# Graph network kernel: the first adjacency matrix built slab by slab beside its first product, the second one made by turning tiles on TensorE

## What is computed

```python
edge_index = jnp.stack([src, dst])
x = _layernorm(x + _L0_gnn_ref(...))   # 3 times: m = h @ weight[i]; agg = segment_sum(m[src], dst); h = gru_cell(agg, h)
x = _layernorm(x + _L1_gnn_ref(...))   # hypergraph: sums of h[src] at dst, then of those at src, batch norm
x = _layernorm(x + _L2_gnn_ref(...))   # attention: softmax over the edges of a src, sum of attn * mapped[dst] at src
x = _layernorm(x + _L3_gnn_ref(...))   # an MLP on each edge, segment sum at dst, an MLP on each node
```

## Time and profile before

| | |
|---|---|
| median of three executions | 5898.96 us (5894.77 to 5907.12) |
| profiled execution | 5895.11 us, of which the span from first to last instruction is 5893.0 us |
| busy: TensorE, GpSimd, VectorE, ACT | 69 %, 44 %, 38 %, 29 % of the span |
| mean granted TensorE clock | 0.864 of full speed |
| moved by DMA | 786.87 MB |

### The profile page before, as it was taken

The page is one execution under the profiler, slowest core; times in us unless marked ns, Lnnn a source line. Parts: engine busy times, 40 slices in busy tenths (PEclk is TensorE's granted clock), DMA queues, the critical chain, the costliest instruction groups (busy, mean ns, idle before and its releaser), DMA issues. The chain is left out here.

```text
span 5893.0 us, 80722 instructions
## 1 busy us (share of the span) xinstructions
PE 4074.7 (69%) x24696; PEld 3170.2 (54%) x24698; DVE 2255.1 (38%) x4547; ACT 1685.4 (29%) x2823; POOL 2578.0 (44%) x2583
## 2 busy tenths in 40 slices
PE   4960000000999998996999799679999577777777
PEld 2430000000787787874555455369999466666665
DVE  5993000000446446437000100547777633333333
ACT  0020000000555555543000100358877322222222
POOL 0037777777777777760000000000000377777772
PEclk9985555555999999998999899799999799999998
DMA  5929500000883883881666666114543111111111
GB/s 188 407 77 366 209 0 0 0 3 0 275 285 102 274 271 106 286 233 41 195 200 173 160 200 199 44 57 144 148 143 116 43 52 50 51 51 51 50 51 39
DMA packets 307968, 786.87 MB, mean 134 GB/s; under 512 B 100762, under 2 KB 116823, under 8 KB 307783
## 3 DMA queue, kind: packets, MB, share of 16 engines
q1 hardware_dynamic: 182152, 548.50, 30.2%
q10 hardware_dynamic: 43680, 177.21, 7.8%
q0 software_dynamic: 81952, 58.72, 4.5%
HBM read 599.36 MB, written 184.70 MB: 133 GB/s over the span
## 5 line engine op out<-in xcount | busy, mean ns | idle before, releaser
L548 POOL DMA_INDIRECT rows<-table,idx_ring x880 | 871.7, 991 | 2291.2 <-ACT idx_ring L556 2023.4
L1017 POOL DMA_INDIRECT adj_t<-cell_val,cell_at x832 | 811.7, 976 | 637.4 <-DVEq L1705 362.1
L1017 POOL DMA_INDIRECT adj_s<-cell_val,cell_a x832 | 871.0, 1047 | 281.5 <-issue 281.5
L450 PE MATMUL ps<-tiles_r,stage_r 128*128 128x512 f32 x1524 | 605.0, 397 | 285.3 <-ACT tiles_r L406 280.5
L406 ACT CAST tiles_r<-onehot 128x1024 fp32r<-128x1024 f16 x254 | 266.6, 1050 | 1260.3 <-DMA onehot<-adj_t 1065.0
L452 PE MATMUL ps<-tiles_r,lower_r 128*128 128x512 f32 x1524 | 602.5, 395 | 0.0
L1405 PE MATMUL ps<-ident,big 128*128 128x128 f32 x14 | 3.2, 425 | 714.1 <-DVE big L1813 714.1
L459 PE MATMUL ps<-big,onehot 128*128 128x387 bf16 x2695 | 461.6, 329 | 47.8 <-DMA onehot<-adj_s 42.6
L459 PE MATMUL ps<-big 128*128 128x387 bf16 x2695 | 459.0, 328 | 42.7 <-DMA big<-adj_t 39.1
L597 PE MATMUL ps<-rows,ident 128*128 128x128 f32 x1760 | 397.2, 310 | 131.6 <-DMA rows<-table,idx_ring 99.5
L450 PEld LDWEIGHTS ps<-tiles_r,stage_r 128*128 128x128 f32 x1524 | 290.4, 191 | 354.4 <-issue 281.6
(11 more groups left out here) (355 smaller groups left out, 6491.4 us busy)
## 6 DMA issues: line engine op xcount, KB each, us to landing
onehot<-adj_t SPq DMA_DIRECT2D x338, 512.0 KB, 4.5
big<-adj_t SPq DMA_DIRECT2D x338, 512.0 KB
onehot<-adj_s SPq DMA_DIRECT2D x170, 512.0 KB, 3.6
adj_t<-rows ACTq DMA_DIRECT2D x13, 6656.0 KB, 46.8
adj_s<-rows ACTq DMA_DIRECT2D x13, 6656.0 KB, 53.8
big<-adj_s SPq DMA_DIRECT2D x84, 512.0 KB
x_fm<-adj_s SPq DMA_DIRECT2D x84, 512.0 KB
rows<-table,idx_ring POOLq DMA_INDIRECT x880, 2.5
```

The costliest lines, as they stand in the source:

```text
L450: nc.tensor.matmul(psum_fm(p, n)[:, 0:cut], upper_rows[:, k, :], tile[:, 0:cut], start=k == 0, stop=False, skip_group_check=True)
L548: nc.gpsimd.indirect_dma_start(rows[:, s, 0:P], None, table[0:N, :], bass.IndirectOffsetOnAxis(idx_ring[:, s:s + 1], 0),).then_inc(row_lan ...
L1017: nc.gpsimd.indirect_dma_start(out, bass.IndirectOffsetOnAxis(cells[:, c:c + 1], 0), cell_val[:, c:c + 1], None).then_inc(S(f"{name}{2 * c ...
```

## The change

It changes the first stage and pass 0; passes 1 to 5 and the later stages keep their work.

- The edges lie in eight **slabs** (`SL`) of 13,312 edges, 104 on each partition. Slab after slab goes through compare, addresses and scatter, so that GpSimd scatters slab `n` while VectorE and TensorE compare slab `n + 1`.
- A compare instruction takes 12 distances at once (`SHIFTS`), 12 x 104 = 1,248 elements, 24 of them for a slab; the distance grows from 276 to 288. For each, TensorE issues three matmuls of 416 columns and twelve of 104 columns.
- The zeros of `adj_t` are written in three sets, and a slab's scatter waits for the set that it needs (`need`, worked out from the counts of destinations). Of `adj_s` neither zeros nor scatter are left.
- Pass 0 (`first_sp`, `first_act`, `first_pe`, `first_dve`) starts a group as soon as the slabs that write it are done (`slab_done`). TensorE also turns each tile's 16 blocks of 128 by 128 (`turn_over`), VectorE copies the turned tile to SBUF (`turned_out`) and SP stores it into `adj_s`. ACT alone casts the tile for the products. The three last row blocks, which need the result of the last group, come in 13 turns behind (`rows_behind`).

```diff
-RUN = 277
+RUN = 289
...
+SL = 8
+SLW = EC // SL
+SLE = P * SLW
+SHIFTS = 12
+TRIES = HALO // SHIFTS
...
+ZEROED = [(GROUPS - 1, 0, 1), (2, 3, 4, 5), (6, 7, 8, 9, 10, 11)]
...
-            sp.dma_start(edge_x[:, 1:EC + 1], in_order).then_inc(S("ordered_in"), 16)
-            sp.dma_start(edge_x[1:P, 0:1], in_order[0:P - 1, EC - 1:EC], allow_slow_non_contiguous=True)\
...
+            sp.dma_start(edge_x[:, :, 1:SLW + 1], in_order).then_inc(S("ordered_in"), 16)
+            sp.dma_start(edge_x[1:P, :, 0:1], in_order[0:P - 1, :, SLW - 1:SLW], allow_slow_non_contiguous=True)\
...
-            for q in range(2):
-                sp.wait_ge(S(f"at_written{q}"), 16 * EC // 2)
-            sp.wait_ge(S("at_ext"), 16 * EXT_BLOCKS)
             for p in range(GRU_LAYERS):
-                matrix_sp(p, sp)
+                matrix_sp(p, sp) if p else first_sp(sp)
...
+            def same_keys(n):
+                for r in range(TRIES):
+                    done = TRIES * n + r
+                    wait(dve, S("same_used"), done - 3)
+                    own = keyx[:, n, 0:SLW]
+                    behind = keyx[:, n, SHIFTS * r + 1:SHIFTS * r + 1 + SLW]
+                    nc.vector.tensor_tensor(eq[done % 4], own.unsqueeze(1).to_broadcast([P, SHIFTS, SLW]),
+                                            bass.AP(behind.tensor, behind.offset, [behind.ap[0], [1, SHIFTS], [1, SLW]]),
                                             ALU.is_equal).then_inc(S("same_ready"), 1)
...
+                        for m in range(0, SHIFTS, 4):
+                            added(4 + n % 2, slice(0, 4 * SLW), ident_h[:, :], eq[u][:, m:m + 4, :].rearrange("p m c -> p (m c)"))
+                        for m in range(SHIFTS):
+                            last = added(6 + n % 2, bass.ds(SHIFTS * r + m + 1, SLW), ident_h[:, :], eq[u][:, m, :])
...
+            for n in range(SL):
+                pool.wait_ge(S("cells_ready"), n + 1)
+                if n < 2:
+                    zeroed(GROUPS + n)
+                if n == 2:
+                    pool.wait_ge(S("zeroed"), len(ZEROED))
...
+                for c in range(SLW):
+                    if n and c == SC:
+                        slab_written(n - 1)
+                    scatter_cells(adj_t, cell_at, f"at_written{n % 2}", n * SLW + c)
...
+            for turn in range(FIRST_TURNS):
+                g, t, blocks = tile_of(turn)
+                if turn == PASS_TURNS:
+                    sp.wait_ge(S("at_ext"), 16 * EXT_BLOCKS)
+                elif t == 0 and g < GROUPS - 1:
+                    sp.wait_ge(S("slab_done"), sp.value_load(need[0:1, g:g + 1], min_val=1, max_val=SL))
+                elif t == 0:
+                    sp.wait_ge(S("slab_done"), SL)
+                load(turn, g, t, blocks)
+                if turn > RING:
+                    store(turn - RING - 1, *tile_of(turn - RING - 1))
...
+            def turn_over(turn, more, blocks):
+                wait(pe, S("cast_dve"), turn - 1 + more)
+                raw = raw_tile(0, turn % RING)
+                for m in range(*blocks):
+                    for j in range(KT):
+                        last = nc.tensor.transpose(flips[turn % 2][:, j, m, :], raw[:, m * GW + j * P:m * GW + (j + 1) * P],
+                                                   ident_c[:, :])
+                last.then_inc(S("turned"), 1)
```

More of the change, by code:

```diff
@@ L381, in matrix_sp, with landed, first_sp, load @@
             matrix(sp, p, body)
-        def landed(eng, first_turn, t, i):
+        def landed(eng, first_turn, t, i, step=STEP):
             turn = first_turn + t
-            eng.wait_ge(tile_landed[turn % RING], 16 * (turn // RING + 1) + 16 * (STEP // RING) * i)
+            eng.wait_ge(tile_landed[turn % RING], 16 * (turn // RING + 1) + 16 * (step // RING) * i)
+        ALL, HEAD, REST = (0, KT), (0, 1), (1, KT)
+        def first_sp(sp):
+            tiles = adj_t[0:CELLS, :].rearrange("(r c) a -> r (c a)", c=ROW)
+            tiles_s = adj_s.rearrange("(r c) a -> r (c a)", c=ROW)
+            def load(turn, g, t, blocks):
+                wait(sp, S("cast_act"), turn - RING + 1)
+                wait(sp, S("turned"), turn - RING + 1)
+                span = slice(blocks[0] * GW, blocks[1] * GW)
+                sp.dma_start(raw_tile(0, turn % RING)[:, span], tiles[g * P:(g + 1) * P, t * TW:(t + 1) * TW][:, span]
+                             ).then_inc(tile_landed[turn % RING], 16)
+            def store(turn, g, t, blocks):
+                sp.wait_ge(S("cast_dve"), turn + 1)
+                out = tiles_s[t * P:(t + 1) * P, g * TW:(g + 1) * TW].rearrange("r (j m c) -> r j (m c)", j=KT, m=KT)
+                span = slice(blocks[0] * P, blocks[1] * P)
+                sp.dma_start(out[:, :, span], turned[turn % RING].rearrange("p j m c -> p j (m c)")[:, :, span]
+                             ).then_inc(turned_stored[turn % RING], 16)
+            def tile_of(turn):
+                if turn >= PASS_TURNS:
+                    return turn - PASS_TURNS, TURNS - 1, REST
+                return turn // TURNS, turn % TURNS, ALL if turn % TURNS < TURNS - 1 else HEAD
+            sp.wait_ge(S("need_ready"), 1)
+            for turn in range(FIRST_TURNS):
[9 more added lines that the diff above has]
+                    store(turn - RING - 1, *tile_of(turn - RING - 1))
+            for turn in range(FIRST_TURNS - RING - 1, FIRST_TURNS):
+                store(turn, *tile_of(turn))
+            for s in range(RING):
+                sp.wait_ge(turned_stored[s], 16 * -(-(FIRST_TURNS - s) // RING))
@@ new lines, in first_act, with cast, body, rows_behind @@
+        def first_act(act):
+            def cast(turn, more, blocks):
+                wait(act, S("tile_used"), turn - RING + 1 + more)
+                s, span = turn % RING, slice(blocks[0] * GW, blocks[1] * GW)
+                nc.scalar.copy(tile_r[s][:, span], raw_tile(0, s)[:, span]).then_inc(S("cast_act"), 1)
+            def body(n, g, first_turn, i):
+                for t in range(TURNS):
+                    landed(act, first_turn, t, i)
+                    cast(first_turn + t, STEP * i, ALL if t < TURNS - 1 else HEAD)
+            def rows_behind(n, g, turn, i):
+                landed(act, turn, 0, i, LOOPED)
+                cast(turn, LOOPED * i, REST)
+            first_pass(act, body)
+            first_pass_ext(act, rows_behind)
@@ L612, in edge_dve @@
         def edge_dve(dve):
[L613 to L614 removed]
+            chain(dve)(nc.vector.memset(acc[:, :], 0.0))
             def hots(c, h):
@@ L1719, in _ @@
-            dve.sem_inc(S("cells_ready"), 1)
-            cells(cell_a2[:, :], src_s, col_v)
+            step(nc.vector.tensor_tensor(ext_i[:, 24:24 + SL], where, unused, ALU.add))
             dve.sem_inc(S("cells_ready"), 1)
```

559 lines of the change are left out of this document (353 added, 206 removed).

## The result

| | before | changed |
|---|---|---|
| median | 5903.04 us (5894.77 to 5908.85, 4 runs) | 5539.17 us (5531.08 to 5546.52, 4 runs) |
| profiled execution, of which span | 5895.11, 5893.0 us | 5546.52, 5544.8 us |
| mean granted clock of TensorE | 0.864 | 0.913 |
| first scatter transfer | 371.3 us | 167.9 us |
| last transfer of `adj_t` ends | 1476 us | 1309.5 us |

The ratio is 0.9384, 95 % interval 0.9365 to 0.9403: 364 us faster in the median, 349 in the profiled executions. I had forecast 5662 us, a gain of 237.

What follows compares the result with a forecast made beforehand. Bound: load, compare, scatter in series until 1476 us, then TensorE. Earlier scatter start 193 us, pass 0 behind it 159 saved, slower scatter 115 lost: 237 off the profiled 5895.1, 5662 us in the median; range 5555 to 5800.

Steps and rivals of the forecast that it cites:

- GpSimd then gets one transfer for each compare instruction: Scatter beside the compares of slabs 1 to 7: 168 compare instructions, 193 transfers counted with the windows between, up to 542 us.
- I take 1.9, ... for the 20 turns with registers: Compare turn: 1.9 us for 20 turns, 1.4 for the other four, 44 us for a slab (34 to 80).
- Its traffic slows the scatter: Scatter beside pass 0: 1.32 us a transfer for the last 434 (1.27 to 1.43), 573 us, ending at 1398 us.
- I take 3.2: Pass 0: 3.2 us a tile, up to 4 with poor overlap; 46.5 tiles behind the scatter take 149 us.
- The way to the first compare: Start of the first stage: 12 us more for single-number loads and 6 for other work, first compare at 111 us.
- Taking it away is worth nothing in itself: Scatter into `adj_s` beside passes 0 to 2: removing it alone gains nothing, as TensorE bounds those passes.
- everything behind 1801.4 us keeps its work: From the first GRU instruction on: the work stays as it was, so only the end of pass 0 moves.
- VectorE paces the compare: Rival on the compare turn: 1.4 us with TensorE's registers hidden, scatter from 168 to 1318, 5582 us; chance 0.17.
- Shut out: Rival beside compares: GpSimd gets no transfer in, 5796 us; chance 0.20 shared with a 2.5 us turn, 5758 us.
- Half clock: Rival in pass 0: TensorE at 1.2 GHz, 5.4 us a tile, 5884 us, or 5748 at 4.6 us; chance 0.10.
- The ring of four: Rival in pass 0: loads, stores and copies wait for the tile four back, 5.6 us a tile, 5917 us; chance 0.05.
- The overlap does not happen: Rival: pass 0 begins only when the first stage is over, at 1398 us, giving 6054 us; chance 0.02.

Runs made afterwards that it cites:

- held_back: The changed kernel with pass 0 held back until all eight slabs are written: 5896.78 us, ratio 0.9994 to the kernel before.
- shifts24: The changed kernel with two compare instructions joined into one of 2,496 elements, twelve for a slab: 5670.77 us.
- cast_beside: The changed kernel with one more VectorE cast, SBUF to SBUF, for each tile of pass 0, into a tile nobody reads: 5555.15 us.
- shifts8: The changed kernel with 8 distances in a compare instruction instead of 12, 832 elements, 36 for a slab: 5512.89 us.
- turned_twice: The changed kernel with each of the sixteen turns of a pass 0 tile made twice into the same place: 5573.48 us.
- halo_between: The changed kernel with the first set of zeros in place and the other two behind the halo of slabs 1 to 7: 5539.43 us.

## Why the prediction was wrong in its size

**Which step failed.** The structure held: the chain (load, compare, scatter, and then the tail of pass 0) is the one that ends last, held_back shows that the overlap carries all of it, and passes 1 to 5 keep their time to within 4 us. Four terms of the sum were mis-sized, all too dear, and one more was called zero.

- *"GpSimd then gets one transfer for each compare instruction"* was right where I used it (shifts24, timeline), and what I put into it was wrong: "I take 1.9, ... for the 20 turns with registers". TensorE's turn is 1.78 us on the mean of a loop, midway between its columns' 1.2 and 2.3, since registers and matmuls overlap in part. That is not far from 1.9. What I left out is that VectorE, whose instructions the transfers meet, doesn't go at TensorE's pace: the ring of four compared tiles, with the first turns quick, lets it run twelve to fifteen instructions at 1.37 us before it meets TensorE. So a slab's compare is 37 us on VectorE and not 44, and then VectorE waits 5.7 us for TensorE's last turns before it makes the addresses in 6.6. A slab takes 50 us, as forecast, but GpSimd runs nearly free in 12 of them and not in 6. 416 transfers in 581.5 us are 1.40 us each; I had 1.56. This term is half of the error, 58 us even with a stand of 7.8 in it.
- *"Its traffic slows the scatter"* was a wrong cause here. The earlier trace rows has 70 transfers in 100 us of pass 0 and 79 alone, and I gave the difference to the traffic, with VectorE's casts named beside it. By the rows under cast_beside some 60 % of it are casts, which have left VectorE, and the rest is one stand of 4.9 us. The 74 beside the zeros were one stand too, of 7.4 us. So traffic lengthens no transfer; it lengthens the stands (3.0 us without it, 4.9 and 7.4 with it), and in the scatter of the changed kernel there are none but that at slab 1. Why they are gone stays open. 21 us.
- *"I take 3.2"* for a tile. TensorE alone sets it, 0.88 us of turns and 1.94 of products and no wait, 2.82 us; the estimate by columns, 0.054 a turn, was right and I left it for a middle. Three resources near one another (TensorE 2.82, DMA share 1.01) did not add up. 46.5 x 0.38 = 18, and the 17 us around it were 10: 25 us together. By the Trainium skill (TensorE: Matmul & The Clock Gate, "Back-to-back issue gap"), with its 81 ns for a pair, the turns of a tile would take an estimated 1.3 us. Here they take 0.88, so on this point the measurement decides.
- *The way to the first compare*, "I take 12" for the single numbers, came out 6 us shorter (104.8, not 111). VectorE starts on the edges at 72.5 us, 3.2 later than before and not 12; the loads are issued 2.8 us earlier, so the single numbers cost about 6. The rest of the way costs 8.2 us more, where I had 6. With the slab's compare 7 us shorter and 3 us lost in the steps from the compare's end to the first transfer it is 10 us.
- *"Taking it away is worth nothing in itself"* is wrong by 33 us in the kernel before. The changed kernel has the gain in its third GRU stage too: from the GRU's start to the load of pass 4 it is 12.7 us faster. But the edge stage, from the first to the last gather, is 13.5 us slower (1151.1 against 1137.6). These two happen to cancel, which made "everything behind 1801.4 us keeps its work" come out to 2.4 us.

**Rivals.** *VectorE paces the compare* (5582 us) was the nearest: its start of 168 and its scatter end of 1318 are what happened to 0.1 and 9 us, though VectorE paces half of the turns only. The start is luck, a first compare 6 us earlier and 6 us more behind it; the compares themselves ended at 598 and not 462, as the halo held slab 1 back for 86 us and each slab took 50. *Shut out* did not occur: where compares stand without a gap, a transfer gets in at the end of each one (of every second in shifts8). *Half clock* did not occur: the granted clock was 1.00 in every full stretch of pass 0, with turned_twice also. The Trainium skill (TensorE: Matmul & The Clock Gate, Part 4) says that turns do not count for the clock as products do; beside products, these runs show no cost of that. *The ring of four*: TensorE never waited in a full stretch. *The overlap does not happen*: its 6054 us was too dear as well; held_back is 5897.

**The range** left out what its own bounds allowed. I took a value above the lower bound in each of the terms, and all of these bounds are what a resource does when nothing interferes. Together they are 168 + 850 x 1.27 + 46.5 x 2.7 + 17 = 1390 for the GRU's start, 5488 us in the median. The low end of 5555 lay 27 us under the nearest rival, room for one more term at its bound and not for several at once.

**What stays open.** Why the edge stage takes 1151 us in the changed kernel and 1138 in the one before, with the same code: its 880 gathers last 1006 instead of 991 ns on the mean, 981 in shifts8 (1131 us), and up to 1162 us in other kernels here. The phase of GpSimd against VectorE is a guess; no run tests it. The difference moves medians by up to 20 us and hides gains of that size, as for halo_between.

## What to carry to other kernels

- Beside VectorE, GpSimd's indirect transfers go at the rate of VectorE's instructions with two inputs in SBUF: one input in PSUM gives it its own pace back (1.27 us), while joining them into longer ones is a loss (132 us here). Shorter ones helped only where gaps stood between them; without gaps a transfer took two of them, 1.87 us. Read the length of single transfers, not the count in a stretch, before a slowing is put down to traffic.
- An overlap is worth what it hides and not what it starts earlier: holding pass 0 back gave back the whole gain of 364 us. Behind the overlap only the tail counts, and its rate is that of one resource.
- A small transfer behind big ones on the same engines can wait 86 us; give it its place between two sets of them. Ahead of all of them it delays what they feed.

## Of the hardware, not expected

- An indirect transfer ends 0.84 us behind the end of the compare that holds it up, for instructions spaced 0.94, 1.37, 1.68 and 3.4 us alike. It takes at least 0.97 us and the next follows 0.30 us later, so one fits into every compare when these are 1.37 us apart, and only into every second at 0.94 us without gaps.
- A VectorE copy of 2,048 numbers out of PSUM (1.22 us) and a compare with one input in PSUM (1.44 us) lengthen no transfer; a cast from SBUF to SBUF of 0.59 us lengthens it to 1.25 us, though it has one input.
- With the DMA engines full (share 1.01, 370 GB/s) indirect transfers are issued as fast as without traffic, every 1.27 us. What traffic lengthens is the stands between them, where there are any: 3.0 us without, 7.4 us beside the zeros.
